# A graph-transformer layer: mixer coefficients taken four pairs at a time, closing blocks reordered, TensorE loops in the first stage, two table comparisons on GpSimd

## The chip, the cores and the metric

One core of one Trainium2 chip runs the whole program. The metric is the device time in microseconds of one execution, the median of the runs. Before the change it is 474.52 us (three runs, 474.12 to 474.85). The profiler took one further execution: it took 474.66 us, and its span from first to last instruction is 472.9 us.

## The reference, cut to what matters

N = 384 nodes, D = 1024 features, 16 heads of 64, 12288 edges. All tensors are float32. Three blocks are computed from the same normalised input:

```python
xn = layernorm(x)
# 1: graph attention
q, k, v = xn @ wq.T + bq, xn @ wk.T + bk, xn @ wv.T + bv
q2, k2, v2 = heads(q @ wiq.T + biq), heads(k @ wik.T + bik), heads(v @ wiv.T + biv)
mask = full((N, N), -inf); mask[src, dst] = softplus(w)[type - 1]; mask[i, i] = w3 where it is -inf
attn = softmax(q2 @ k2.T / 8 + mask)
gnn = (attn @ v2) @ wo.T + bo
# 2: mixer
f(x) = exp(-x * x / 2)
coeff = sum over the 64 columns of a head of f(xn @ Wq + bq) * f(xn @ Wk + bk)
mix = (coeff * (xn @ Wv + bv)) @ Wo + bo
# 3: feed-forward with one chosen expert, on layernorm(x + gnn + mix)
```

## The kernel before, in words

Every float32 product is made of three TensorE products of rounded halves: high part of the weights by high part of the data, high by low, low by high. ScalarE makes the high part of a weight block (`split_hi`), VectorE the low part (`split_weights`), and SyncE loads the blocks (512 KB each) into a ring of slots (`load_weights`). A semaphore for each slot says that its high part is there (`hi_ready`), its low part (`lo_ready`), and that TensorE is done with it (`w_used`).

TensorE works through a fixed order of jobs, written out by hand:

- The first stage has 32 column jobs (`column_job`: 24 matmuls of 128x128 by 128x384): q, k, v from the input, then q2. Each job takes one slot of four and one PSUM bank of four, and waits for its bank (`bank_free`), `hi_ready` and `lo_ready`. All of it is unrolled. ScalarE and VectorE empty the banks; VectorE also looks for double edges, and GpSimd scatters the edge values into four tables in DRAM (`tables`).
- The v2 stage has eight row blocks and one column job for k2. At its end the four tables come back into SBUF: table 0 becomes the mask, and VectorE merges the other three into it (`merge_table`: a comparison of 1152 columns that finds the entries present, then a predicated copy).
- Eight pairs of heads follow (`pair(j)` on ScalarE and VectorE, the loop over j on TensorE). TensorE does `scores(j)` (18 matmuls with 64 rows), `pv(j-1, 0)` (6 matmuls), three column jobs in banks 0 and 1, `pv(j-1, 1)`, the column job of the mixer's values (`rv`), and `coefficients(j)`: two matmuls of a block matrix of ones (`head_ones`) by the high and the low part of the features, into bank 0. The features of a pair are one tensor: ScalarE squares q and k of the mixer (`square`), VectorE adds them, ScalarE takes exp (line 702) and its high part (704), VectorE the low part (1103). ScalarE empties the value job (`mix_value`, 718), VectorE multiplies by the coefficients in PSUM (1108), ScalarE and GpSimd split the product into the halves `T2` (733 and 469). The last scores of a pair wait for `mix_value`, the `pv` for the low part of the turned probabilities (`turned_lo`, 1041), and the first column job of the pair for the product (`mix_ready`), since it uses bank 0.
- The closing stage has two halves of eight row blocks. In each the blocks b = 0 to 3 take the mixer's data (`T2`), 4 to 7 the attention's (`T0`). Block 0 of the first half lies inside the last pair, and `pv(7, 0)` and `pv(7, 1)` lie behind blocks 1 and 2. SyncE loads the four first blocks of the feed-forward weights (`E_USES`) between these, and GpSimd loads x again (509).
- The feed-forward stage and the output follow, which the change leaves as they are.

## Time and profile before

| what | value |
|---|---|
| median of 3 runs | 474.52 us (474.12 to 474.85) |
| profiled execution | 474.66 us, span 472.9 us |
| TensorE matmul busy | 465.9 us (99%) |
| VectorE busy | 342.3 us (72%) |
| ScalarE busy | 262.2 us (55%) |
| GpSimd busy | 157.2 us (33%) |
| granted TensorE clock | 1.000 |
| DMA | 91.92 MB, 194 GB/s |

The page gives the busy time of each engine and a chain of work followed back from the last instruction. The end of a matmul is modelled, so two neighbouring matmuls overlap in the record: what one costs is the distance of the starts, not its duration. An idle time stands in brackets behind a row, with what ended it.

### The profile page before, as it was taken

Reading aid. Unit: us, or ns where it says so; the run is one execution under the profiler, and the core shown is the slowest. Engines: PE = TensorE matmul, PEld = TensorE weight load, DVE = VectorE, ACT = ScalarE, POOL = GpSimd, SP = SyncE. Lnnn points to the kernel's source line nnn. Section 1 sums busy time; section 2 is a strip of 40 time slices with the busy share of each in tenths; the row PEclk is TensorE's granted clock in tenths of the full one; section 3 lists DMA queues with packets and bytes.
Section 4 is the critical chain, followed back from the end, with each engine's and each line's share of the span. In section 5 each row is a group of like instructions: output and inputs, shape, how many; then the busy total and the mean of one; then the engine's idle time right before and its main releaser. Section 6 shows DMA issues by size and latency. Waiting matters only on the chain.

```text
span 472.9 us, 7361 instructions
## 1 busy us (share of the span) xinstructions
PE 465.9 (99%) x2533; PEld 432.4 (91%) x2533; DVE 342.3 (72%) x796; ACT 262.2 (55%) x429; POOL 157.2 (33%) x176
## 2 busy tenths in 40 slices
PE   7999999999999999999999999999999999999996
PEld 5999999999999888999999999999998888888885
DVE  6979966677626259687978888796966794587294
ACT  3734433333324245788989889897974542163170
POOL 3147677777767741002130202212142000050200
PEclk9999999999999999999999999999999999999999
DMA  8877756655444454577675766766679835210463
GB/s 243 325 230 230 239 195 167 176 182 180 154 152 153 133 200 179 175 226 253 205 232 184 235 192 197 247 180 224 192 240 382 308 115 179 89 46 0 155 247 133
DMA packets 39049, 91.92 MB, mean 194 GB/s; under 512 B 7410, under 2 KB 20306, under 8 KB 38884
## 3 DMA queue, kind: packets, MB, share of 16 engines
q1 hardware_dynamic: 33604, 83.15, 54.0%
q0 software_dynamic: 4832, 7.45, 4.7%
q10 hardware_dynamic: 576, 0.85, 0.5%
q8 instruction: 20, 0.33, 0.3%
q14 instruction: 17, 0.14, 0.1%
HBM read 77.96 MB, written 13.47 MB: 193 GB/s over the span
## 4 chain that ended last, share of the span: by engine, by line
PE 87%; DVE 5%; DMA 3%; ACT 3%; issue 1%; SPq 0%; DVEq 0%; ACTq 0%
PE PS L1278 32%; PE PS L1288 28%; PE PS L1283 16%; PE PS L1416 3%; PE PS L1404 2%; DMA turn<-U 2%; PE PS L1535 2%; PE PS L1346 2%; DMA U<-x 1%; DVE U L1076 1%; DVE w_lo L895 1%; PE PS L1266 1%; ACT U L659 1%; PE PS L1539 1%; ACT w_hi L536 1%
## 5 line engine op out<-in xcount | busy, mean ns | idle before, releaser
L895 DVE TENSOR_TENSOR w_lo<-raw,w_hi 128x1024 fp32r<-128x1024 f32 x86 | 104.4, 1225 | 45.0 <-ACT w_hi L536 45.0
L536 ACT ACTIVATE w_hi<-raw 128x1024 fp32r<-128x1024 f32 x87 | 90.8, 1054 | 68.5 <-PE PS L1288 44.1
L454 POOL DMA_INDIRECT table<-evalue,where x96 | 103.0, 1073 | 45.7 <-issue 25.2
L1283 PE MATMUL PS<-xT_hi,w_lo 128*128 128x384 f32 x320 | 61.9, 334 | 0.0
L1278 PE MATMUL PS<-xT_hi,w_hi 128*128 128x384 f32 x320 | 61.9, 334 | 0.0
L1278 PE MATMUL PS<-xT_lo,w_hi 128*128 128x384 f32 x320 | 61.9, 334 | 0.0
L1278 PEld LDWEIGHTS PS<-xT_lo,w_hi 128*128 128x128 f32 x320 | 56.0, 188 | 0.0
L1278 PEld LDWEIGHTS PS<-xT_hi,w_hi 128*128 128x128 f32 x320 | 56.0, 188 | 0.0
L1283 PEld LDWEIGHTS PS<-xT_hi,w_lo 128*128 128x128 f32 x320 | 56.0, 188 | 0.0
L469 POOL TENSOR_TENSOR T_lo<-U,T_hi 128x384 fp32r<-128x384 f32 x8 | 8.2, 1020 | 97.8 <-ACT T_hi L733 97.8
L1288 PE MATMUL PS<-w_hi,T_hi 128*128 128x512 f32 x144 | 40.0, 391 | 0.0
L1288 PE MATMUL PS<-w_hi,T_lo 128*128 128x512 f32 x144 | 39.8, 389 | 0.0
L950 DVE SCALAR_TENSOR_TENSOR U<-U,V,cst 128x128 f32<-128x128 f32 x96 | 33.6, 350 | 6.0 <-DMA U<-key_dram 3.7
L1288 PE MATMUL PS<-w_lo,T_hi 128*128 128x512 f32 x144 | 37.8, 389 | 0.0
L598 ACT ACTIVATE T_hi<-PS,bias 128x384 fp32r<-128x384 f32 x24 | 13.8, 576 | 41.7 <-PE PS L1283 41.7
L1288 PEld LDWEIGHTS PS<-w_hi,T_lo 128*128 128x128 f32 x144 | 27.0, 188 | 5.7
L1288 PEld LDWEIGHTS PS<-w_lo,T_hi 128*128 128x128 f32 x144 | 27.0, 188 | 5.6
L1288 PEld LDWEIGHTS PS<-w_hi,T_hi 128*128 128x128 f32 x144 | 27.0, 188 | 5.2
L1076 DVE STREAM_TRANSPOSE U<-U 128x384 f32<-128x384 f32 x48 | 24.0, 551 | 10.5 <-DMA turn<-U 10.5
L659 ACT ACTIVATE U<-U,nmax 128x384 f32<-128x384 f32 x48 | 28.9, 605 | 3.7 <-DVE nmax L1064 3.7
L965 DVE SCALAR_TENSOR_TENSOR T_lo<-PS,bias,T_hi 128x384 fp32r<-128x384 f32 x24 | 14.8, 615 | 16.1 <-ACT T_hi L598 16.1
L666 ACT ACTIVATE U<-U,rsum 128x384 f32<-128x384 f32 x48 | 25.8, 604 | 0.0
(241 smaller groups left out, 817.1 us busy)
## 6 DMA issues: line engine op xcount, KB each, us to landing
raw<-weights SPq DMA_DIRECT2D x84, 512.0 KB, 4.6
turn<-U SPq DMA_DIRECT2D x16, 576.0 KB, 4.0
U<-turn SPq DMA_DIRECT2D x64, 144.0 KB, 2.9
U<-key_dram SPq DMA_DIRECT2D x32, 192.0 KB, 4.1
mask<-weights SPq DMA_DIRECT2D x9, 512.0 KB, 5.1
table<-Q POOLq DMA_DIRECT2D x4, 576.0 KB, 9.5
V<-conv SPq DMA_DIRECT2D x4, 512.0 KB, 5.4
U<-table POOLq DMA_DIRECT2D x3, 576.0 KB, 7.5
```

The lines of the kernel that those rows point to most:

```text
L454: pool.indirect_dma_start(tables[g], bass.IndirectOffsetOnAxis(ap=where[:, k:k + 1], axis=0), evalue[:, k:k + 1], None, bounds_check=N * N ...
L536: act.activation(w_hi[slot][:], raw[slot][:], ACT.Copy).then_inc(hi_ready[slot], 1)
L659: act.activation(prob[:, h, t, :], prob[:, h, t, :], ACT.Exp, bias=nmax[:, h, t:t + 1], scale=SCALE, accum_out=ssum[:, h, t:t + 1]).then_i ...
L666: act.activation(prob[:, h, t, :], prob[:, h, t, :], ACT.Copy, scale=rsum[:, h, t:t + 1]).then_inc(prob_ready, 1)
L895: dve.tensor_tensor(w_lo[slot][:], raw[slot][:], w_hi[slot][:].bitcast(F32), ALU.subtract).then_inc(lo_ready[slot], 1)
L950: dve.scalar_tensor_tensor(out=key_junk, in0=key_row[:, s, c * P:(c + 1) * P], scalar=ekey[:, ch0 + c:ch0 + c + 1], in1=tri, op0=ALU.is_eq ...
L965: dve.scalar_tensor_tensor(out=dst[1][:, j, :], in0=PS[:, A_BANKS[a % 4], 0:N], scalar=bias[:, a:a + 1], in1=dst[0][:, j, :].bitcast(F32), ...
L1076: dve.transpose(blocks.rearrange("p (c m t i) -> p t m c i", c=NQ, m=NT, t=NT)[:, t], prob[:, h, t, :].rearrange("p (m c i) -> p m c i", m ...
L1278: pe.matmul(o, w_hi[slot][:, k * P:(k + 1) * P], src[part][:, k, :], start=(k == 0 and part == 0), stop=False)
L1283: last = pe.matmul(o, wl, src[0][:, k, :], start=False, stop=(k == KB - 1))
L1288: return pe.matmul(bank, src[part][:, 2 * kp + k2, t * P:(t + 1) * P], weights_in[slot][:, k2 * HALF:(k2 + 1) * HALF], start=start, stop=stop)
L1416: last = pe.matmul(PS[:, 7, 0:N], vs[:, m, h, :], probT[part][:, m, :], start=(m == 0 and part == 0), stop=(m == NT - 1 and part == 1))
```

## The change

1. The coefficients are computed for four pairs at once (`GROUP` = 4). The mixer's columns (Wq, Wk, Wv, their biases, and the rows of Wo) are laid out in another order on the host, so that a block of 128 columns holds 16 columns of each of eight heads, and four blocks hold eight heads whole. VectorE adds up the features of the four blocks (`feat_sum`), and `head_ones` has groups of 16 in place of 64. High part, low part and the two matmuls are done for j = 3 and j = 7 alone. The values of the pairs are kept (`raw_value`), and VectorE multiplies all four in a row behind the coefficients. The splits of the products come four pairs later, the last four in the closing stage.
2. In the closing stage the first half takes its blocks in another order, the feed-forward weights are loaded and split two blocks later, behind a wait for all of the mixer's products, and GpSimd loads x ahead of the last four low parts.
3. Jobs 4 to 31 of the first stage are two loops on TensorE with four jobs in the body (five rounds and two), whose waits compare with a register.
4. The comparisons for tables 1 and 2 are done on GpSimd (`is_gt` for `not_equal`), into two buffers. VectorE keeps that of table 3 and the three predicated copies.

```diff
+GROUP = 4
+SHARE = HD // GROUP
+C_ORDER = (((1, 0), (1, 1), (0, 0), (0, 1), (0, 2), (1, 2), (1, 3), (0, 3)),
+           ((1, 0), (1, 1), (1, 2), (1, 3), (0, 0), (0, 1), (0, 2), (0, 3)))
...
+        feat_sum = v2_rows[:, :, 0:P]
+        def raw_value(j):
+            return v2_rows[:, :, j * P:(j + 1) * P] if j else mix_v.rearrange(rows_of_three, t=NT)
...
             for b in range(5, 16):
                 load_weights(*C_USES[b], weights[72 + b])
-                if b == 5:
-                    sp.wait_ge(vs_ready, KB)
                 if b == 7:
+                    sp.wait_ge(ml_ready, KB)
                     sp.wait_ge(score_read, KB * 6 + 1)
-                if 5 <= b < 9:
-                    load_weights(*E_USES[(b - 5)], weights[72 + 16 + (b - 5)])
+                if 7 <= b < 11:
+                    load_weights(*E_USES[(b - 7)], weights[72 + 16 + (b - 7)])
...
+            for g in range(STREAMS - 2):
+                pool.wait_ge(table_in[g], 16)
+                if g == 0:
+                    pool.wait_ge(dup_ready, CH)
+                if g == 1:
+                    pool.wait_ge(diag_step, 2 * NT)
+                pool.tensor_scalar(present[g], later[g], ABSENT, None, ALU.is_gt).then_inc(found, 1)
...
             for j in range(KB):
-                if j:
+                if j >= GROUP:
                     pool.wait_ge(vs_ready, j)
-                    mix_lo(j - 1)
-                    pool.wait_ge(ml_ready, j)
+                    mix_lo(j - GROUP)
+                    pool.wait_ge(ml_ready, j - GROUP + 1)
                 values(j)
...
                 normalise(1)
+                if j >= GROUP:
+                    mix_hi(j - GROUP)
                 if j:
-                    mix_hi(j - 1)
-                    act.wait_ge(feat_ready, j)
+                    act.wait_ge(feat_exp, j)
+                if j > 1:
+                    act.wait_ge(feat_added, adds(j - 1))
                 square(sq_q, 1, 6, rq)
...
                 act.wait_ge(sq_summed, j + 1)
-                act.activation(sq_q, sq_q, ACT.Exp, scale=-0.5).then_inc(feat_exp, 1)
-                act.wait_ge(feat_exp, j + 1)
-                act.activation(feat[0], sq_q, ACT.Copy).then_inc(feat_hi, 1)
+                if j == 0:
+                    act.wait_ge(vs_ready, 1)
+                if j == GROUP:
+                    act.wait_ge(feat_ready, 1)
+                act.activation(sq_q.rearrange(rows_of_three, t=NT) if j % GROUP else feat_sum,
+                               sq_q.rearrange(rows_of_three, t=NT), ACT.Exp, scale=-0.5).then_inc(feat_exp, 1)
                 split_hi(*ahead[3])
+                if j % GROUP == GROUP - 1:
+                    act.wait_ge(feat_added, adds(j))
+                    act.activation(feat[0].rearrange(rows_of_three, t=NT), feat_sum, ACT.Copy).then_inc(feat_hi, 1)
                 turned_hi(j, 0)
+                mix_value(j, rv)
                 if j:
                     out_hi(j - 1)
-                mix_value(j, rv)
...
             for j in range(KB):
                 pair(j)
-            mix_hi(KB - 1)
             split_hi(*C_USES[2])
             split_hi(*C_USES[3])
             pv_copy(KB - 1, 0)
             turned_hi(KB - 1, 1)
+            for j in range(KB - GROUP, KB):
+                mix_hi(j)
             split_hi(*C_USES[4])
...
             def merge_table(g):
-                dve.wait_ge(table_in[g], 16)
-                dve.tensor_scalar(present, later[g], ABSENT, None, ALU.not_equal).then_inc(mask_step, 1)
-                dve.wait_ge(mask_step, 2 * g + 1)
+                if g < STREAMS - 2:
+                    dve.wait_ge(found, g + 1)
+                else:
+                    dve.wait_ge(table_in[g], 16)
+                    dve.tensor_scalar(present[0], later[g], ABSENT, None, ALU.not_equal).then_inc(found, 1)
+                    dve.wait_ge(found, g + 1)
...
-                dve.wait_ge(feat_hi, j + 1)
-                dve.tensor_tensor(feat[1], sq_q, feat[0].bitcast(F32), ALU.subtract).then_inc(feat_ready, 1)
+                if j % GROUP:
+                    dve.wait_ge(feat_exp, j + 1)
+                    if adds(j) > 1:
+                        dve.wait_ge(feat_added, adds(j) - 1)
+                    dve.tensor_tensor(feat_sum, feat_sum, sq_q.rearrange(rows_of_three, t=NT),
+                                      ALU.add).then_inc(feat_added, 1)
                 split_weights(*ahead[3])
+                if j % GROUP == GROUP - 1:
+                    dve.wait_ge(feat_hi, j // GROUP + 1)
+                    high, low = (f.rearrange(rows_of_three, t=NT) for f in feat)
+                    dve.tensor_tensor(low, feat_sum, high.bitcast(F32), ALU.subtract).then_inc(feat_ready, 1)
                 turned_lo(j, 0)
-                dve.wait_ge(coeff_done, j + 1)
-                dve.wait_ge(mixv_ready, j + 2)
-                dve.tensor_tensor(mix_v, PS[:, 0, 0:N], mix_v, ALU.mult).then_inc(mix_ready, 1)
+                if j % GROUP == GROUP - 1:
+                    dve.wait_ge(coeff_done, j // GROUP + 1)
+                    dve.wait_ge(mixv_ready, j + 2)
+                    for i in range(j - GROUP + 1, j + 1):
+                        dve.tensor_tensor(raw_value(i), PS[:, 0, 0:N].rearrange(rows_of_three, t=NT), raw_value(i),
+                                          ALU.mult).then_inc(mix_ready, 1)
...
-            for a in range(2, FIRST):
-                pe.wait_ge(bank_free[a % 4], a // 4 + 1)
-                column_job(*A_USES[a], T0 if a >= 3 * KB else xT, A_BANKS[a % 4])
+            for a in (2, 3):
+                pe.wait_ge(bank_free[a], 1)
+                column_job(*A_USES[a], xT, A_BANKS[a])
+            for src, begin, end in ((xT, 1, 3 * KB // 4), (T0, 3 * KB // 4, FIRST // 4)):
+                with pe.Fori(0, end - begin) as i:
+                    for s in range(4):
+                        pe.wait_ge(bank_free[s], i + (begin + 1))
+                        column_job(A_SLOTS[s], i + begin, src, A_BANKS[s])
...
-                    pe.wait_ge(mix_ready, j + 1)
+                    if j % GROUP == 0:
+                        pe.wait_ge(mix_ready, j + 1)
+                    else:
+                        pe.wait_ge(sq_done, 2 * j)
                     column_job(*slot_use(rk), T1, 0)
...
-                pe.wait_ge(sq_done, 2 * j + 2)
-                coefficients(j)
+                if j % GROUP == GROUP - 1:
+                    pe.wait_ge(sq_done, 2 * j + 2)
+                    coefficients(j)
...
-                    pe.wait_ge(ol_ready if b >= 4 else ml_ready, 2 * (b % 4) + 2)
-                    row_block(*uses[b], T2 if b < 4 else T0, banks, b % 4, b == 0, b == 7)
+                    mixer, kp = C_ORDER[half][b]
+                    pe.wait_ge(ml_ready if mixer else ol_ready, 2 * kp + 2)
+                    row_block(*uses[b], T2 if mixer else T0, banks, kp, b == 0, b == 7)
```

## Rows read from the trace of the kernel before

**Rows 1.** Part 1 of the page: busy time, share of the span, instructions.
```profile
PE 465.9 (99%) x2533; PEld 432.4 (91%) x2533; DVE 342.3 (72%) x796; ACT 262.2 (55%) x429; POOL 157.2 (33%) x176
```

**Rows 2.** Stretches: length, busy time of each engine, clock, DMA share, GB/s.
```profile
23.00:147.00 124.00, 124.00 (x716) 123.74 (x715) 88.01 (x281) 46.37 (x61) 85.77 (x80) 1.00 0.61 188
...
203.75:225.25 21.50, 21.29 (x130) 20.53 (x130) 18.65 (x43) 19.09 (x37) 2.67 (x4) 1.00 0.70 227
225.25:246.30 21.05, 21.05 (x129) 20.55 (x128) 17.70 (x42) 18.23 (x36) 4.37 (x5) 1.00 0.68 215
...
330.52:351.86 21.34, 21.23 (x123) 19.90 (x123) 17.57 (x41) 18.11 (x36) 4.49 (x5) 1.00 0.68 217
```

**Rows 3.** One line's instructions: least, median, greatest duration in ns, first and last start.
```profile
L1425 PE MATMUL PS<-T_lo,head_ones x8: 338/338/339, 203.5 to 351.7; 128*128 128x384 f32 x8
```

**Rows 4.** Timeline around the end of pair 3: start us, duration us, engine, line.
```profile
242.41 0.53 ACT L702 ACTIVATE U<-U 128x384 f32<-128x384 f32 x1
...
243.40 1.05 ACT L536 ACTIVATE w_hi<-raw 128x1024 fp32r<-128x1024 f32 x1
...
244.48 1.23 DVE L895 TENSOR_TENSOR w_lo<-raw,w_hi 128x1024 fp32r<-128x1024 f32 x1 [0.39 <-ACT w_hi L536]
...
245.62 1.35 DVE L1041 TENSOR_TENSOR probT_lo<-U,probT_hi 128x1152 fp32r<-128x1152 f32 x1
...
246.04 0.34 PE L1425 MATMUL PS<-T_lo,head_ones 128*128 128x384 f32 x1
...
246.06 0.58 ACT L718 ACTIVATE U<-PS,bias 128x384 f32<-128x384 f32 x1
...
247.01 0.56 DVE L1108 TENSOR_TENSOR U<-PS,U 128x384 f32<-128x384 f32 x1
...
247.46 0.35 PE L1404 MATMUL PS<-T_hi,q_hi 64*128 64x384 f32 x2
...
247.49 0.55 DVE L1060 CUSTOM_DVE_ANT_0 U<-PS,mask 128x384 f32<-128x384 f32 x1
...
249.24 1.55 PE L1278 MATMUL PS<-T_hi,w_hi 128*128 128x384 f32 x8
```

**Rows 5.** Timeline at the start of pair 7, where TensorE waits twice.
```profile
331.96 0.18 PEld L1404 LDWEIGHTS PS<-T_hi,q_hi 64*128 64x128 f32 x2 [0.44 <-ACT U L718]
...
332.69 0.19 PEld L1416 LDWEIGHTS PS<-probT_hi,vs 128*128 128x128 f32 x1 [0.26 <-DVE probT_lo L1041]
```

**Rows 6.** Merge of the tables: timeline rows, two lines' durations, landings of the tables.
```profile
179.09 0.75 DVE L986 TENSOR_SCALAR U<-U 128x1152 f32<-128x1152 f32 x1
...
184.64 1.55 DVE L988 COPY_PREDICATED mask<-U 128x1152 f32<-128x1152 uint32 x1
...
190.82 1.55 PE L1278 MATMUL PS<-xT_hi,w_hi 128*128 128x384 f32 x8
...
L485 POOL CAST vs<-V x8: 503/503/1260, 185.6 to 347.7; 128x384 fp32r<-128x384 f32 x8
...
DMA to landing us min/median/max: 5.0/7.1/10.1
```

**Rows 7.** First stage: a sequencer's wait, chain, fetch queue, two small transfers to landing.
```profile
L1275 PEldq EVENT_SEMAPHORE  x1: 51/51/51, 36.5 to 36.5; - x1
...
39.78 2.77 PE PS L1278 x16
...
q8 instruction: 20, 0.33, 0.3%
...
U<-down_b SPq DMA_DIRECT2D x1, 0.2 KB, 2.4
...
bias<-bias_cols SPq DMA_DIRECT2D x1, 36.0 KB, 4.3
```

**Rows 8.** Closing stage: last low part of the attention, a weight split that waits.
```profile
364.22 1.01 POOL L476 TENSOR_TENSOR T_lo<-U,T_hi 128x384 fp32r<-128x384 f32 x1 [7.69 <-ACT T_hi L738]
...
369.07 1.06 ACT L536 ACTIVATE w_hi<-raw 128x1024 fp32r<-128x1024 f32 x1 [3.65 <-DMA raw<-weights]
```

More of the change, by code:

```diff
@@ L58, with adds @@
 DEPTH = len(A_SLOTS) - 1
+def adds(j):
+    return j - j // GROUP
 def slot_use(r):
@@ L132, in gps_layer @@
         later = [U[:, g * NT * N:(g + 1) * NT * N].rearrange("p (t n) -> p t n", t=NT) for g in range(STREAMS - 1)]
-        present = U[:, 4608:4608 + NT * N].rearrange("p (t n) -> p t n", t=NT)
+        present = [U[:, c:c + NT * N].rearrange("p (t n) -> p t n", t=NT) for c in (3456, 4608)]
         prob = U[:, 0:2 * NT * N].rearrange("p (h t n) -> p h t n", h=2, t=NT)
@@ L250, in gps_layer @@
         mask_step = sem("mask_step")
+        found = sem("found")
         v_copied = sem("v_copied")
@@ L277, in gps_layer @@
         feat_exp = sem("feat_exp")
+        feat_added = sem("feat_added")
         feat_hi = sem("feat_hi")
@@ L464, in _ @@
                     table_in[g - 1] if g else first_mask_in, 16)
+            for g in range(STREAMS - 2):
[5 more added lines that the diff above has]
+                pool.tensor_scalar(present[g], later[g], ABSENT, None, ALU.is_gt).then_inc(found, 1)
             def mix_lo(j):
                 pool.wait_ge(mh_ready, j + 1)
-                pool.tensor_tensor(T2[1][:, j, :], mix_v, T2[0][:, j, :].bitcast(F32),
+                high, low = (T2[c][:, j, :].rearrange(rows_of_three, t=NT) for c in range(2))
+                pool.tensor_tensor(low, raw_value(j), high.bitcast(F32),
                                    ALU.subtract).then_inc(ml_ready, 1)
@@ L502, in _ @@
                     pool.dma_start(row_bo, rows[0:2, :].partition_broadcast(P)).then_inc(rows_in, 16)
-            mix_lo(KB - 1)
-            pool.wait_ge(ml_ready, KB)
             pool.wait_ge(pT_ready, KB * 2 - 1)
             pool.wait_ge(block_ready, KB * 6)
-            pool.wait_ge(feat_ready, KB)
+            pool.wait_ge(feat_ready, KB // GROUP)
             pool.dma_start(x_rows, x.rearrange("(t p) d -> p t d", p=P)).then_inc(xr_in, 16)
+            for j in range(KB - GROUP, KB):
+                mix_lo(j)
+                pool.wait_ge(ml_ready, j + 1)
             out_lo(KB - 1)
@@ L714, in mix_value @@
                 act.wait_ge(w_used[slot], use + 2)
-                if j:
-                    act.wait_ge(ml_ready, j)
-                act.activation(mix_v, PS[:, 1, 0:N], ACT.Identity,
+                act.wait_ge(vs_ready, j + 1)
+                act.activation(raw_value(j), PS[:, 1, 0:N].rearrange(rows_of_three, t=NT), ACT.Identity,
                                bias=bias[:, 8 * KB + j:8 * KB + j + 1]).then_inc(mixv_ready, 1)
@@ L732, in mix_hi @@
                 act.wait_ge(mix_ready, j + 2)
-                act.activation(T2[0][:, j, :], mix_v, ACT.Copy).then_inc(mh_ready, 1)
+                act.activation(T2[0][:, j, :].rearrange(rows_of_three, t=NT), raw_value(j),
+                               ACT.Copy).then_inc(mh_ready, 1)
             def out_hi(j):
@@ L747, in _ @@
             turned_hi(KB - 1, 1)
+            for j in range(KB - GROUP, KB):
+                mix_hi(j)
             split_hi(*C_USES[4])
@@ L766, in _ @@
                 split_hi(*C_USES[b])
-                if 6 <= b < 10:
-                    split_hi(*E_USES[b - 6])
+                if 8 <= b < 12:
+                    split_hi(*E_USES[b - 8])
                 if b == 10:
@@ L1152, in _ @@
                     add_rows(1)
-                if 6 <= b < 10:
-                    split_weights(*E_USES[b - 6])
+                if 8 <= b < 12:
+                    split_weights(*E_USES[b - 8])
                 if b == 9:
@@ L1566 @@
     v2, k2 = halves(a["gnn_wiv"].T), columns(a["gnn_wik"].T)
-    mixer = [columns(a["mix_" + n]) for n in ("Wq", "Wk", "Wv")]
+    lane = np.arange(P)
+    turned = np.concatenate([(2 * GROUP * (j // GROUP) + lane // SHARE) * HD + SHARE * (j % GROUP) + lane % SHARE
+                             for j in range(KB)])
+    mixer = [columns(a["mix_" + n][:, turned]) for n in ("Wq", "Wk", "Wv")]
     pairs = [v2[0:4], k2[0:1], v2[4:8]]
@@ L1571 @@
     pairs += [mixer[n][KB - 1:KB] for n in (1, 0, 2)]
-    wo, mo = halves(a["gnn_wo"].T), halves(a["mix_Wo"])
-    outs = [mo[0:4], wo[0:4], mo[4:8], wo[4:8]]
+    wo, mo = halves(a["gnn_wo"].T), halves(a["mix_Wo"][turned])
+    outs = [(wo, mo)[mixer][4 * half + kp:4 * half + kp + 1] for half in range(2) for mixer, kp in C_ORDER[half]]
     weights = np.concatenate(first + pairs + outs + [halves(a["ffn_base_W"].T)])
@@ L1596 @@
         "disc": disc.transpose(3, 0, 1, 2),
-        "bias_cols": np.concatenate([a[n].reshape(KB, P) for n in names]).T,
+        "bias_cols": np.concatenate([(a[n][turned] if n.startswith("mix") else a[n]).reshape(KB, P)
+                                     for n in names]).T,
         "rows": np.stack([a["gnn_bo"], a["mix_bo"], a["ffn_base_b"]]),
```

14 lines of the change are left out of this document (7 added, 7 removed).

## The prediction

> **What bounds the kernel now.** I read the busy times first: TensorE works for 465.9 of 472.9 us [rows 1]; the next engine is VectorE with 72%. Then the stretches. In the whole unrolled first stage TensorE is never idle (124.00 of 124.00), and a regular pair of heads, from its first score matmul to that of the next, takes 21.05 us with no idle time [rows 2]. Two pairs are longer, 21.50 and 21.34 us. The timeline shows why: at the start of pair 7 TensorE waits 0.44 us for the emptied value bank (line 718) and then 0.26 us for the low part of the turned probabilities (line 1041) [rows 5]; pair 1 begins with the same two waits, shorter ones (two borders of eight). So the kernel is bound by the number of matmuls, with some tenths lost at two borders. An edit gains if it takes matmuls away, and gains nothing if it only relieves another engine; it loses when it makes TensorE wait.
>
> **Part 1, grouped coefficients.** Two matmuls of each of the 16 go away for six of eight pairs: 12 matmuls. The line with the low features has eight of them, of 338 ns [rows 3], but these overlap: sixteen matmuls of the same shape take 2.77 us in the chain, 0.173 us each [rows 7]. 12 x 0.173 = 2.08 us, all on TensorE's path, since nothing hides there. Gain 2.08 us.
>
> What the removed matmuls covered: the scores now start 0.35 us earlier after the value job, and their last third waits for line 718, the `pv` for line 1041. At the border of pairs 3 and 4 line 718 begins at 246.06 and is done at 246.64, and the last third of the scores begins at 247.46: 0.8 us of slack, 0.5 when TensorE comes 0.35 earlier. Line 1041 ends at 246.97, and the six matmuls of the `pv` before the column job of 249.24 begin near 248.1, 1.1 us behind that [rows 4]. So in the regular pairs nothing is late. At pairs 1 and 7 the `pv` already waits for line 1041. That line comes earlier as well: ScalarE no longer copies the high features (between exp and the split of 243.40 [rows 4]) ahead of the weight split that VectorE's split and line 1041 stand behind. Both sides move by 0.35 and about 0.45 us, so 0.1 us is regained at each border: 0.2 us. Bounds: nothing, or the whole excess of these pairs over 21.05, 0.45 + 0.29 = 0.74 us [rows 2].
>
> The groups' ends, j = 3 and 7. The feature chain is longer there: VectorE adds (as long as the 0.56 of line 1108), ScalarE splits the weights and then copies, VectorE splits the weights and then takes the low part. With the rows of pair 3 [rows 4]: ScalarE's split can begin when exp ends, 242.94 in place of 243.40, and ends about 243.95; its copy ends 244.5; VectorE's split, which waits for ScalarE's, runs from 244.0 to 245.2, the low part to 245.7. The second coefficient matmul starts at 246.04: in time by 0.3 us. Line 1041 then runs to 247.0 as before. The four products come at a distance of 0.48 us (247.01 to 247.49): three more are 1.45 us, the last ends at 247.01 + 1.45 + 0.56 = 249.0. TensorE's next column job overwrites the coefficients' bank at 249.24. So it is in time by 0.2 us; at a distance of 0.62 us (one duration and a little) it would wait 0.2 us. I take 0.1 us lost. Queued behind the four products on VectorE is the read of the next scores (line 1060), which begins 1.45 us later; the job that needs those banks starts 4.2 us behind the one at 249.24, so it isn't late. At j = 7 the products stand before the closing blocks, which now want them far later.
>
> VectorE's and ScalarE's work per pair (17.7 and 18.2 of 21.05 us [rows 2]) does not grow: six additions replace six low parts, six copies go.
>
> **Part 2, closing stage.** No matmul is added or taken away. The mixer's blocks 2 and 3 move behind three attention blocks. The last products are ready about 249.0 - 246.04 = 3 us behind the last coefficients; ScalarE takes four high parts only after the splits and `turned_hi` there, and GpSimd four low parts of 1.0 to 1.8 us, the last of them about where the attention's last low part ran before, 364.22 [rows 8]. In the new order the first block that wants them starts 4 x 4.1 us + two `pv` of 1.0 us behind block 1, near 370. SyncE's four loads for the feed-forward come two blocks later. That relieves the stretch in which a split waited 3.65 us for its weights [rows 8], a wait that TensorE didn't feel; the four are needed 45 us later. Behind SyncE's new wait for all products (near 364) stands the load for block 8, needed near 382. I cost all this at nothing; the cover is 5 us at the tightest.
>
> **Part 3, the loops.** The same 28 jobs. The three waits of a job become instructions with registers on TensorE's sequencer. They were satisfied long before, since slots and banks turn over in four jobs. What hides the sequencer's work is its lead: the wait of a job ran at 36.5 us, the job's matmuls began at 39.78 [rows 7], 3.3 us later. Register steps and a branch fit in that lead if the instructions are at hand. I take 0; the other end is a rival below.
>
> **Part 4, comparisons on GpSimd.** VectorE's merges begin at 179.09 and end with the third copy, 184.64 + 1.55 = 186.2; the three comparisons of 0.75 and three copies of 1.55 us fill that time [rows 6]. GpSimd takes 0.50 us for a cast of 384 columns, 1.26 us when it is held up, so 1.5 to 3.8 us for 1152 columns [rows 6]. With 1.5 the entries are found at 180.6 and 182.1, the copies follow, the third table has landed by 173.1 + 10.1 = 183.2, and the merge ends near 186.0. No change; TensorE wants the score banks at 190.82 [rows 6], and six reads of 0.5 us (the distance of line 1060) behind 186.2 end at 189.3. The two comparisons removed from VectorE lie in slack: below nothing this can't go.
>
> The Trainium skill (SBUF — State Buffer, "Practical consequences") says that a VectorE instruction with two SBUF inputs contends with a GpSimd instruction that reads SBUF, and that one of the two blocks fully. The spread of the cast, 503 to 1260 ns, agrees with it [rows 6]; a serial order of these pieces would end the merge 1.5 us later than I wrote, which the slack of 1.5 us nearly covers.
>
> **The sum.** -2.08 - 0.2 + 0.1 = -2.2 us. The profiled execution took 474.66 us (span 472.9): 472.5 us. The median is 0.14 us lower: 472.4 us. About 0.2%, 0.95 us, is what a measurement of this kernel can tell from no change.
>
> **Rival A: the loops fetch again (ends slower).** The instructions come in through a queue of their own: 20 packets, 0.33 MB, so 16 KB each, which is about 256 instructions [rows 7]. One round of the loop has 4 x 48 matmul and weight-load instructions and some 20 others. If the jump back finds its target gone, the sequencer stands until a block has come. A round straddles a border of such blocks in most positions. The price of one fetch: the smallest transfer lands after 2.4 us, one of 36 KB in the busy beginning after 4.3 [rows 7]; a block's packet itself takes 0.3% x 16 x 472.9 / 20 = 1.1 us more. That is 3.5 to 5.4 us, of which the lead hides 3.3. There are five jumps back (4 and 1): 1 to 10 us. At 4.3 us a fetch it is 5.0 us, and the time is 477.4 us. It decides from a fetch of 3.3 us on, and makes the kernel slower than before from 3.8 us. For it: size of body and block, and the trace has no slack in this stage. Against it: the lead, and that nothing here shows whether a block just left stays. It would show as five gaps on TensorE between 31 and 147 us and more packets in that queue.
>
> The Trainium skill (Runtime: NRT & Kernel Launch, "Instruction fetch mechanics") has this rule: prefetch is sequential, and a taken branch to a target outside the two blocks at hand waits for a DMA of it. It also gives TensorE's memory as 2048 instructions, by which the whole body would stay. The page thus speaks for both; no row of before has a branch.
>
> **Rival B: the mask comes late.** If GpSimd needs 2.6 us for a comparison, held up by the copies, entries are found at 181.7 and 184.3 and the merge ends at 188.2, 2 us late. The six reads of scores (0.5 us each) end at 191.3; TensorE waits 0.4 us, and the turned probabilities of pair 0, for which TensorE waited already, come about 1 us later: +1.5 us, 473.9 us. At 3.8 us a comparison TensorE alone waits 3.0 us, 475.4. For it: no slack for VectorE there; against it: the tables' early landing.
>
> **Rival C: the matmuls go and TensorE waits instead.** If the slack of 0.3 us at the ends of the groups or of 0.5 at the borders isn't there, since the strided features and values cost more or the turned probabilities come back late, each border gives back up to 0.35 us. Half of them: +1.0 us, 473.4 us. The rows of pairs 1 and 7 speak for it, the regular pairs against.
>
> **How the numbers follow.** Forecast 0.54, own range 471.6 (the whole 0.74 regained) to 473.1 (nothing regained, 0.5 lost at the groups' ends). Rival A 0.24: mostly slower (0.17), partly within (0.05). Rival B 0.11: mostly within. Rival C 0.11: faster 0.07, within 0.04. Together faster 0.62, within 0.2% 0.19, slower 0.19. The range goes up into rival A to 476.8, which leaves about 0.12 above it and 0.04 below.
>
> **What would show it.** Right: TensorE idle-free from 23 to 147 us; pairs of 20.7 us for j = 0, 1, 2, 4, 5, 6 and four coefficient matmuls in all; the fourth product done before the first column job of pair 4; block 5 of the closing stage without a wait. Wrong: five gaps in the first stage; a merge that ends behind 187.5; TensorE idle before line 1278 at the start of pair 4.

## The result, and the profile after

The changed kernel takes 480.31 us (median of four runs, 478.77 to 483.87), the kernel before 474.33 us beside it: ratio 1.0114, 95% interval 1.0062 to 1.0166. The forecast was 472.4 us with a range up to 476.8, so it was wrong in sign and the time lies outside the range. The ratios here and below are those of the fast executions alone (within 1.5% of the kernel's fastest), so they need not be the ratios of the medians. The profiled execution took 479.62 us, its span is 477.8 us.

Part 1 of the page, and one group of part 5 (busy us and mean ns of one, then the idle time before it):

```profile
PE 464.7 (97%) x2521; PEld 431.2 (90%) x2521; DVE 344.8 (72%) x794; ACT 257.8 (54%) x423; POOL 164.7 (34%) x178
...
L1334 PE MATMUL PS<-xT_hi,w_hi 128*128 128x384 f32 x320 | 63.3, 339 | 4.2 <-DVE smax L1105 4.2
```

TensorE has 12 instructions fewer than in [rows 1], as the change says. But its busy share fell from 99 to 97%: the work went, the time didn't. Nearly all of the new idle time is one wait, for the scores of pair 0. The waits of TensorE (line waited for, total, times, longest):

```profile
PE PS L1334 <- DVE smax L1105: 4.2, 1, 4.2
PE PS L1381 <- DVE w_lo L893: 1.6, 1, 1.6
PE PS L1322 <- ACT U L595: 1.4, 1, 1.4
PE PS L1339 <- DVE probT_lo L937: 0.9, 1, 0.9
...
PE PS L1466 <- ACT U L758: 0.5, 1, 0.5
PE PS L1478 <- DVE probT_lo L1086: 0.2, 1, 0.2
```

The second, third and fourth lie in the first 31 us, and waits at these places stand in most profiles, with and without the change (before has the second and 0.7 us of the third). The timeline of the merge answers to [rows 6]; first GpSimd's instructions with their durations, then VectorE's, then TensorE's:

```profile
L490 POOL TENSOR_SCALAR U<-U x2: 3837/4155/4473, 179.5 to 183.4; 128x1152 f32<-128x1152 f32 x2
...
183.35 1.57 DVE L1033 COPY_PREDICATED mask<-U 128x1152 f32<-128x1152 uint32 x1 [3.03 <-POOL U L490]
187.97 1.88 DVE L1033 COPY_PREDICATED mask<-U 128x1152 f32<-128x1152 uint32 x1 [3.05 <-POOL U L490]
189.89 1.42 DVE L1031 TENSOR_SCALAR U<-U 128x1152 f32<-128x1152 f32 x1
191.34 1.52 DVE L1033 COPY_PREDICATED mask<-U 128x1152 f32<-128x1152 uint32 x1
...
196.15 2.93 PE L1334 MATMUL PS<-xT_hi,w_hi 128*128 128x384 f32 x8 [4.16 <-DVE smax L1105]
198.88 1.66 PE L1334 MATMUL PS<-xT_lo,w_hi 128*128 128x384 f32 x8
```

A comparison takes GpSimd 3.84 and 4.47 us, not 1.5. VectorE stands idle before the first two copies, which wait for GpSimd; the mask is whole at 192.9 us (186.2 before), six reads of scores follow, and TensorE starts again at 196.15. There its first eight matmuls lie 2.73 us apart from the next eight; at full clock that distance is 1.39 us. So a second loss of 1.4 us follows the wait: the granted clock is at its lower level (0.50, 1.2 GHz) behind the idle time. Stretches, with length, busy time of the engines, clock, DMA share and GB/s, the last of them that of the first eight matmuls:

```profile
31.00:158.00 127.00, 127.00 (x721) 125.40 (x721) 88.05 (x277) 48.25 (x64) 93.17 (x87) 1.00 0.61 183
185.78:210.21 24.43, 20.27 (x115) 19.44 (x115) 16.00 (x37) 14.74 (x29) 4.77 (x3) 0.93 0.33 108
210.21:231.96 21.75, 21.03 (x127) 20.15 (x126) 18.34 (x41) 17.97 (x34) 2.19 (x2) 1.00 0.73 230
231.96:252.65 20.69, 20.69 (x127) 20.19 (x126) 17.80 (x42) 17.21 (x34) 2.83 (x3) 1.00 0.70 220
252.65:273.69 21.04, 21.04 (x129) 20.54 (x128) 18.43 (x42) 17.95 (x35) 2.54 (x3) 1.00 0.70 223
...
196.15:198.88 2.73, 2.73 (x8) 2.73 (x9) 2.73 (x6) 2.73 (x10) 0.00 (x0) 0.50 0.16 29
```

The first row is the stretch of the loops: no gap. The next four are pairs 0 to 3, each from its first score matmul to that of the next. Pair 0 is 5.46 us longer than before (18.97), pair 1 0.25 longer, pair 2 0.36 shorter, pair 3 even, pairs 4 to 6 0.3 shorter each, and what follows 0.43 shorter. With 1.00 us by which pair 0 starts later, that is the +5.0 us between the two traces.

### The profile page after: what moved, and what is told of

It reads as the page before. It is cut to its first block, busy times and chain, and to the rows that moved or that the text cites. A ratio compares the mean times of both kernels' runs of the same rounds, so it can differ in the third digit from the quotient of the medians.

```text
span 477.8 us, 7358 instructions
## 1 busy us (share of the span) xinstructions
PE 464.7 (97%) x2521; PEld 431.2 (90%) x2521; DVE 344.8 (72%) x794; ACT 257.8 (54%) x423; POOL 164.7 (34%) x178
## 4 chain that ended last, share of the span: by engine, by line
PE 66%; DMA 12%; issue 8%; POOL 7%; DVE 5%; ACT 0%; POOLq 0%; DVEq 0%; SPq 0%; ACTq 0%
PE PS L1334 24%; PE PS L1344 21%; PE PS L1339 12%; DMA table<-evalue,where 7%; POOL table L471 5%; PE PS L1478 4%; PE PS L1466 2%; POOL U L490 2%; PE PS L1602 2%; DMA turn<-U 1%; DMA key_dram<-V 1%; DVE w_lo L937 1%; DMA raw<-weights 1%; DMA U<-x 1%; DMA U<-key_dram 1%
## 5 line engine op out<-in xcount | busy, mean ns | idle before, releaser
L1334 PE MATMUL PS<-xT_hi,w_hi 128*128 128x384 f32 x320 | 63.3, 339 | 4.2 <-DVE smax L1105 4.2
L1334 PEld LDWEIGHTS PS<-xT_hi,w_hi 128*128 128x128 f32 x320 | 57.1, 191 | 4.5 <-DVE smax L1105 4.5
L512 POOL CAST vs<-V 128x384 fp32r<-128x384 f32 x8 | 5.7, 717 | 75.7 <-PE PS L1478 75.7
```

The source lines that it names most:

```text
L1334: pe.matmul(o, w_hi[slot][:, k * P:(k + 1) * P], src[part][:, k, :], start=(k == 0 and part == 0), stop=False)
```

## The experiments

The experiments ran on five chips. On three of them TensorE is held up in the first stage whatever the kernel: its matmuls come at multiples of 0.7 us for some 20 us, with nothing that the trace shows it to wait for, and the medians of all kernels lie between 496 and 504 us, that of before too. The first eight kernels and the last two ran there. Their total times tell little; their traces do.

### Each part by itself

e1 is the changed kernel with all comparisons on VectorE, e4 also without the loops; e2 is the kernel before with the two comparisons on GpSimd, e3 with the loops.

```diff
  e1, e4 (against after; e4 also has the 28 jobs unrolled)
-                pool.tensor_scalar(present[g], later[g], ABSENT, None, ALU.is_gt).then_inc(found, 1)
...
+                dve.tensor_scalar(present[1], later[g], ABSENT, None, ALU.not_equal).then_inc(found, 1)
  e2 (against before): the same lines the other way round
  e3 (against before)
+            for src, begin, end in ((xT, 1, 3 * KB // 4), (T0, 3 * KB // 4, FIRST // 4)):
+                with pe.Fori(0, end - begin) as i:
```

> The changed kernel with part 4 undone alone: all three comparisons on VectorE again; grouping, closing order and loops stay. Theory M (the mask comes late because a GpSimd comparison takes 3.8 to 4.5 us, and everything that is lost follows from it): the wait of 4.2 us and the half clock behind it go, pair 0 takes about 18.6 us, and the time is 474.3 - 2.1 = 472.2 us, 0.4 to 0.5% below before. Theory L (the loops or the regrouped work also cost time): above 473.5 us.

> The kernel before with part 4 alone: two comparisons on GpSimd, nothing else. Theory M: TensorE waits about 4 us in pair 0, a stretch at half clock follows, and the time is 474.3 + 8.1 = 482 us (480 to 485), with a wide spread. Theory L: a clearly smaller loss, under 3 us, since the rest of the loss would belong to the other parts.

> The kernel before with part 3 alone: 28 jobs of the first stage in two loops on TensorE. Theory M: no gap between the jobs and 474.3 us within 0.1%, with about four packets fewer in the instruction queue. Theory L (each jump back costs time that the one trace did not show): 1 us or more above before.

> Parts 1 and 2 alone: grouped coefficients and the closing order, with the first stage unrolled and the comparisons on VectorE. Theory M: 472.2 us, the same as with the loops. Theory L: faster than the version with loops by what the loops cost. Predicted sum of my steps: 474.3 - 2.2 = 472.1 us.

Ratios to before: e1 1.0099 (1.0039 to 1.0158), e2 0.997 (0.9903 to 1.0037), e3 1.0037 (0.9979 to 1.0095), e4 1.0031 (0.9972 to 1.009). The two theories can't be told apart by these. Taken at their word, the comparisons would be harmless and the rest would cost time. The trace of e1 says why that can't be read so:

```profile
98.27 0.33 PE L1322 MATMUL PS<-xT_lo,probT_hi 128*128 128x384 f32 x1 [0.42 <-issue]
99.00 0.34 PE L1327 MATMUL PS<-xT_hi,probT_lo 128*128 128x384 f32 x1 [0.39 <-issue]
...
PE PS L1322 <- issue: 12.9, 16, 2.0
```

TensorE reaches pair 0 at 204 to 211 us in these runs in place of 185. VectorE's work ahead of the merge comes late with it, and GpSimd's two comparisons are done by then: in e2 at 189.4 and 198.9 us, while VectorE's first copy begins at 199.63 without waiting for GpSimd. The mask is whole at 205.08 us, 1.1 us behind the start of pair 0 (before: 1.4 us), and e2's pair 0 takes 18.97 us, as before, in spite of its comparisons. What does come through is part 1: pairs 2 and 6 take 20.69 to 20.94 us in e1 and e4 and 21.05 to 21.07 us in e2 and e3.

### The same again, matmuls in the gap, one comparison

e5 and e6 repeat e1 and e2. e7 is the changed kernel with 24 matmuls more (4.16 us) where TensorE waited; e8 moves one comparison to GpSimd and not two.

```diff
  e7
+                    if j == 0:
+                        for _ in range(24):
+                            pe.matmul(PS[:, 7, 0:N], head_ones[:], T1[0][:, 0, :], start=True, stop=True)
  e8
-            for g in range(STREAMS - 2):
+            for g in range(STREAMS - 3):
```

> The changed kernel with all three comparisons on VectorE, once more, since on the first chip every kernel, the one before too, lost some 20 us in the first stage at half rate and times could not be told apart. Theory M (all that is lost follows from the late mask): 472.2 us where before takes 474.3, 0.4 to 0.5% faster. Theory L (the loops or the regrouped work cost too): no faster than before.

> The kernel before with the two comparisons on GpSimd alone, once more. Theory M: about 8 us over before (6 to 10), with TensorE waiting about 4 us for the score reads of pair 0. On the first chip pair 0 took 18.97 us, as before, because TensorE came to it 19 us later, and the mask was there: by theory M that is so wherever TensorE is late, by theory L it would be a sign that the comparisons are harmless.

> The changed kernel with 24 more matmuls of 128x128 by 128x384 (4.16 us) into an unused bank where TensorE waits in pair 0; their results are not used. If the half clock behind the wait follows from TensorE's idle time, the clock stays at full and the time falls by 1.4 us or more below the changed kernel, to about 478 us, with a narrower spread, although there is more work. If the clock falls for another reason, the time stays at 480.

> The changed kernel with one comparison on GpSimd (table 1) and two on VectorE. A comparison of 3.8 us ends at 183.3; copy, comparison, copy, comparison, copy on VectorE end near 188.8 in place of 192.9. TensorE then waits about 1.5 us for the score reads. Theory M: 473.5 to 475.5 us, between the version with none (472.2) and the one with two (480). Theory L (the loss is not in the mask): 480.

The medians are 502.72, 502.06, 499.12 and 497.35 us beside 503.82 (484.78 to 507.35) for before: nothing to be told apart, and the gap that e7 was to fill wasn't there. Its pairs 0 and 1 take 22.81 and 20.69 us: 18.65 + 4.16, and no wait at the border of pair 1; that this is so because ScalarE and VectorE had 4 us more is argued, not shown. In e8 the single comparison took 3.56 us:

```profile
189.24 3.56 POOL L490 TENSOR_SCALAR U<-U 128x1152 f32<-128x1152 f32 x1 [4.51 <-DMA U<-table]
```

### The start of the merge held back

To make the lateness a matter of choice, g1 and g2 hold GpSimd's first comparison until the second or third v2 block of the second half is done, d1 does it with VectorE's merge of e1, and f2 is g2 with 36 matmuls more (6.24 us) in the gap. These ran where TensorE was mostly undisturbed (before 479.29 us, 473.95 to 484.52).

```diff
  g2 (g1: V2_JOBS[1][1]; d1: the same wait on dve)
+                if g == 0:
+                    gate_slot, gate_use = slot_use(V2_JOBS[1][2])
+                    pool.wait_ge(w_used[gate_slot], gate_use + 2)
  f2: g2 and the matmuls of e7, range(36)
```

> The chips of the last runs lose 10 to 30 us in the first stage in every kernel, so that TensorE comes to pair 0 long after the tables. Here the mask's lateness is put back relative to TensorE: in the changed kernel the first GpSimd comparison also waits for the end of the third of the last four v2 blocks, 4.1 us before the scores of pair 0. In the changed kernel's first trace the comparisons began 6.3 us before the scores and TensorE waited 4.2 us, with 16.7 us from the first comparison to the restart. Theory M: restart at -4.1 + 16.7 = 12.6 us behind the scores where 6.0 is natural, a wait of 6.5 us, half clock behind it, and a pair 0 of 26 us in place of 18.6. Theory L: pair 0 under 20 us.

> The same, with the first comparison waiting for the second of the last four v2 blocks, 8.2 us before the scores. Theory M: a wait of 2.4 us, pair 0 of 21 to 22.5 us, that is 4 us less than with the later gate, one for one with the gate. Theory L: no difference between the two gates.

> The later gate (4.1 us before the scores) with all three comparisons on VectorE. Merges of 7.1 us and reads of 3.2 us end 6.3 us behind the scores, where 6.0 is natural. Theory M: a wait of at most 0.5 us and a pair 0 of about 19 us at full clock: the engine that compares decides, not when the tables are there. If the lateness of the tables mattered by itself, pair 0 would be as long as with the comparisons on GpSimd.

> The later gate on GpSimd with 36 more matmuls (6.24 us) into an unused bank in the wait; their results are not used. If the half clock comes from TensorE's idle time, pair 0 takes 18.6 + 6.5 = 25.1 us at full clock and the restarted job's first eight matmuls keep a distance of 0.173 us, against 0.32 to 0.34 and 26.4 us without the filler. If not, both are alike.

Measured: g2 484.42 us, ratio 1.0159 (1.01 to 1.0219); g1 481.75, 1.0091 (1.0048 to 1.0135); d1 477.58, 0.9992 (0.9951 to 1.0033); f2 480.02, 1.0044 (1.0004 to 1.0083). d1 is as fast as before although its TensorE waits 1.3 us for the mask and 1.4 us for a weight split behind VectorE's late work: what parts 1 to 3 give is used up by it. In the profiles of d1 and f2 the added wait does bind (the first comparison begins 3.9 and 3.8 us ahead of pair 0's scores, where the gate was set). In those of g1 and g2 it doesn't: the tables landed later still. The row names the transfer as the releaser:

```profile
183.30 8.14 POOL L493 TENSOR_SCALAR U<-U 128x1152 f32<-128x1152 f32 x2 [4.24 <-DMA U<-table]
...
199.48 2.93 PE L1337 MATMUL PS<-xT_hi,w_hi 128*128 128x384 f32 x8 [7.49 <-DVE smax L1108]
202.21 2.28 PE L1337 MATMUL PS<-xT_lo,w_hi 128*128 128x384 f32 x8
204.33 1.57 PE L1342 MATMUL PS<-xT_hi,w_lo 128*128 128x384 f32 x8
```

So both profiles are repeats of the changed kernel in an execution where the tables came late, the two gates can't be compared as meant, and the wait is 7.5 us (7.6 in g1). The 16 matmuls behind it take 4.85 us in place of 2.77, a loss of 2.1 us to the lower clock. f2 tests just that: with 6.24 us of matmuls more its median is 4.4 us below g2's, and TensorE restarts at full clock and without a wait:

```profile
191.95 6.40 PE L1517 MATMUL PS<-T_hi,head_ones 128*128 128x384 f32 x36
198.19 1.57 PE L1337 MATMUL PS<-xT_hi,w_hi 128*128 128x384 f32 x8
199.60 1.55 PE L1337 MATMUL PS<-xT_lo,w_hi 128*128 128x384 f32 x8
```

The lower clock comes from the idle time: with the gap filled the granted clock stays at 1.00. How much of the 4.4 us is the clock and how much the earlier tables of f2's executions this pair doesn't separate.

### The parts once more, on a chip that was not held up

The changed kernel, e1, e4 and e2 again, side by side; before took 477.83 us (474.73 to 482.6, 29 runs).

> The changed kernel itself, beside its parts on one chip. Theory: the comparisons on GpSimd cost 4.2 us of idle TensorE time at the start of pair 0 and 1.4 us of halved clock behind it, the grouped coefficients give 2.1 us back, and some tenths are lost at pair 1. Expected 478 to 480 us where before takes 474.3, 3.5 to 5 us above before on the same chip. Rival (the one slow read of one execution): the loss is another one in each execution, and the time stands within 2 us of before.

> Changed kernel with the comparisons of tables 1 and 2 back on VectorE, all else kept. Theory (part 4 alone makes the loss): 2 to 2.5 us below before on the same chip, some 472.3 us, where TensorE works undisturbed; and 5.5 to 7 us below the changed kernel. Rival (grouping delays the tables or pair 1 as well): 473.5 to 475 us, nothing gained over before.

> Only the grouped coefficients and the reordered closing blocks: no loops, comparisons on VectorE. Theory: loops are worth nothing either way, so within 0.5 us of the kernel with loops. Rival A (loops wait for instructions): 1 to 10 us faster than the kernel with loops.

> The kernel before with the two comparisons moved to GpSimd and nothing else. Theory: the wait of 4.2 us ahead of the first probability-side column job of pair 0 and the halved clock behind it come alone, so 5 to 6.5 us above before, about 480 us. Rival (the wait needs the grouping, whose pair 0 is shorter by 0.35 us): under 1 us above before.

| kernel | median us (runs) | ratio to before | tables asked for at | mask whole at | wait | pairs 0 to 3 |
|---|---|---|---|---|---|---|
| before (first profile) | 474.52 (3) | | 170.7 | 186.2 | 0 | 82.58 |
| after (first profile) | 480.31 (4) | 1.0114 (1.0062 to 1.0166) | 173.0 | 192.9 | 4.2 | 87.91 |
| h1, all parts | 481.25 (12) | 1.0072 (1.0032 to 1.0111) | 175.6 | 195.6 | 8.0 | 92.25 |
| h2, comparisons back | 476.16 (12) | 0.9969 (0.9924 to 1.0015) | 173.3 | 187.5 | 0 | 85.67 |
| h3, parts 1 and 2 alone | 474.33 (12) | 0.9953 (0.9909 to 0.9997) | 174.7 | 191.8 | 4.3 | 87.04 |
| h4, comparisons alone | 483.16 (6) | 1.0112 (1.0056 to 1.0168) | 176.3 | 196.9 | 7.8 | 92.10 |

The last four columns come from the profile of each, one execution. The rows for h4, and for h3, where VectorE does all three comparisons:

```profile
176.26 0.82 POOL L464 DMA_DIRECT2D mask<-table  x1 [1.88 <-DMA table<-evalue,where]
...
183.80 8.33 POOL L474 TENSOR_SCALAR U<-U 128x1152 f32<-128x1152 f32 x2 [4.41 <-DMA U<-table]
...
200.18 2.93 PE L1291 MATMUL PS<-xT_hi,w_hi 128*128 128x384 f32 x8 [7.83 <-DVE smax L1073]
```

```profile
174.66 0.80 POOL L480 DMA_DIRECT2D mask<-table  x1 [1.86 <-DMA table<-evalue,where]
...
183.96 0.75 DVE L1019 TENSOR_SCALAR U<-U 128x1152 f32<-128x1152 f32 x1
184.75 1.57 DVE L1021 COPY_PREDICATED mask<-U 128x1152 f32<-128x1152 uint32 x1
186.35 0.90 DVE L1019 TENSOR_SCALAR U<-U 128x1152 f32<-128x1152 f32 x1
187.29 2.24 DVE L1021 COPY_PREDICATED mask<-U 128x1152 f32<-128x1152 uint32 x1
...
195.07 2.93 PE L1322 MATMUL PS<-xT_hi,w_hi 128*128 128x384 f32 x8 [4.31 <-DVE smax L1093]
```

Three things follow. The comparisons alone make the whole loss: h4 is 5.3 us above before (2.7 to 8.0), and taking them back from h1 to h2 gives 5.1 us. Parts 1 and 2 without them are faster than before, by 2.2 us (0.1 to 4.3): the amount forecast, if with a wide interval, and h3 beats both kernels. (With the loops as well, h2's gain can't be told from none, and its median of 476.2 us missed the 472.3 expected.) And the merge had no slack to give in the first place: GpSimd asks for the tables, behind its last scatters, at 170.7 us in the profile of before and at 173 to 176 us in the others. From there the mask takes 14.1 to 17.1 us with VectorE's comparisons and 19.9 to 20.6 with GpSimd's. h3's execution came late enough that TensorE waited 4.3 us without any comparison on GpSimd. The runs of before on this chip stand in two groups, 15 from 474.7 to 477.8 and 14 from 479.6 to 482.6 us, about the price of that wait and its clock. The mean granted clock of the runs divides them in the same way: 0.998 to 1.000 in the 15, 0.991 to 0.996 in the 14; the profiled execution of h3, with its wait, has 0.995. I take the late tables for the cause, but no profile of such a run of before was made. What makes the scatters end early or late stays open.

The groups also tell what the parts do. h3's runs divide likewise, seven from 472.6 to 474.4 us (clock 0.998 to 1.000) and five from 477.2 to 479.6 (0.993 to 0.995). Their medians, 474.0 and 478.2, lie 1.9 and 2.5 us below those of before, 475.9 and 480.7: the gain of parts 1 and 2 is there in either group, and isn't a matter of how many runs fell into which. And all 18 runs of h1 and h4 have a clock of 0.996 or less: with the comparisons on GpSimd every execution shows the mark of the wait, without them (before, h2, h3) 20 of 53 do. The first comparison of the two kernels was made against four runs of before that all lie at 474.1 to 474.9 us, which would explain that its distance, 6.0 us, is larger than the one here, 3.4.

Lateness that doesn't show as a wait for the mask comes out at the borders: h2 has none of the first, but pairs 1 to 3 take 22.1 to 22.3 us. Pairs 1 and 2 wait 0.9 us each for the emptied value bank, pair 3 waits 0.8 us at its second coefficient matmul, and h1 has that last wait too. A row of h2, pair 1, then one of h1, pair 3:

```profile
206.91 0.45 PE L1454 MATMUL PS<-T_hi,q_hi 64*128 64x384 f32 x2 [0.91 <-ACT U L749]
```

```profile
276.53 0.44 PE L1487 MATMUL PS<-T_lo,head_ones 128*128 128x384 f32 x1 [0.81 <-DVE T_lo L1157]
```

### What a comparison costs GpSimd, and the loops again

i1 is e3 again. i2 is the kernel before with twelve GpSimd operations more in the closing stage.

```diff
+            for n in (1152, 384):
+                src, dst = U[:, 3840:3840 + n], U[:, 4992:4992 + n]
+                step_m(pool.tensor_scalar(dst, src, ABSENT, None, ALU.is_gt))
+                step_m(pool.tensor_scalar(dst, src, ABSENT, None, ALU.mult))
+                step_m(pool.tensor_copy(dst, src))
+                step_m(pool.tensor_tensor(dst, src, src, ALU.subtract))
+                step_m(pool.memset(dst, 0.0))
+                step_m(pool.tensor_scalar(dst, src, ABSENT, None, ALU.is_gt))
```

> The kernel before with the loops alone. Theory: the loops cost and give nothing, TensorE has no gap from 32 to 147 us, four packets fewer in the instruction queue; time within 1 us of before on the same chip. Rival (the median of the kernel with loops stood 1.8 us above that of the one without): 1 to 2 us above before, with idle time of TensorE or later starts of the scatters on GpSimd.

> The kernel before with twelve more GpSimd operations in the closing stage, where GpSimd has nothing to do: comparison, multiplication by a constant, copy, subtraction, memset, comparison, each on 1152 and then on 384 columns of SBUF. Theory (a comparison costs GpSimd some 3.8 us for 1152 columns by itself, as any operation with arithmetic does; a cast is not a measure of it): comparisons of 3.8 us and 1.3 us, multiplication the same, copy 1.2 to 1.5 us and 0.5 us. Rival (VectorE held GpSimd up in the merge): a comparison of 1.5 us here, where VectorE is idle for long.

Both ran on a chip that holds TensorE up, so i1 (501.75 us beside 498.57, 480.85 to 502.47) settles nothing on time; it has 16 packets of instructions, as every kernel with the loops. i2, by line, busy us and mean ns:

```profile
L529 POOL TENSOR_SCALAR U<-U 128x1152 f32<-128x1152 f32 x1 | 4.0, 4010 | 0.1
L525 POOL TENSOR_SCALAR U<-U 128x1152 f32<-128x1152 f32 x1 | 3.8, 3770 | 0.1
L524 POOL TENSOR_SCALAR U<-U 128x1152 f32<-128x1152 f32 x1 | 3.2, 3156 | 0.1
L527 POOL TENSOR_TENSOR U<-U 128x1152 f32<-128x1152 f32 x1 | 3.0, 2961 | 0.1
...
L524 POOL TENSOR_SCALAR U<-U 128x384 f32<-128x384 f32 x1 | 1.8, 1787 | 0.1
L526 POOL COPY U<-U 128x1152 f32<-128x1152 f32 x1 | 1.8, 1782 | 0.1
```

A comparison of 1152 columns takes 3.2 to 4.0 us, a multiplication as long, a subtraction 3.0, a copy 1.8. The rival of 1.5 us is out. VectorE was busy beside them, so these aren't GpSimd's times undisturbed. f2 has one that is: VectorE was idle from 181.43 us on, and the first comparison, begun at 182.07, took 3.15 us. First f2's two comparisons and VectorE's rows about the first, then the row of the changed kernel just ahead of its own:

```profile
L493 POOL TENSOR_SCALAR U<-U x2: 3148/3798/4447, 182.1 to 185.3; 128x1152 f32<-128x1152 f32 x2
...
180.20 1.23 DVE L940 TENSOR_TENSOR w_lo<-raw,w_hi 128x1024 fp32r<-128x1024 f32 x1
185.25 1.54 DVE L1036 COPY_PREDICATED mask<-U 128x1152 f32<-128x1152 uint32 x1 [3.83 <-POOL U L493]
...
179.09 1.23 DVE L937 TENSOR_TENSOR w_lo<-raw,w_hi 128x1024 fp32r<-128x1024 f32 x1
```

What goes beyond 3.15 us is time for which VectorE was already at work. In the changed kernel its weight split still had 0.84 us to run when the first comparison began, and its predicated copy 1.52 us when the second did: these took 3.84 and 4.47 us, 0.7 and 1.3 more than 3.15. h1 and h4 show the same (3.77 and 3.79 us beside 0.77 and 0.80 us left of the split, 4.46 beside the copy). So 6.3 of the 8.3 us are GpSimd's own, and 2.0 are VectorE in its way.

## Why the prediction was wrong

**The step that failed** is the duration in part 4: "So 1.5 to 3.8 us for 1152 columns. With 1.5 the entries are found at 180.6 and 182.1". They were found at 183.3 and 187.9. Of the 5.8 us by which the second is late, 5.3 are the two durations (3.3 GpSimd's own price, 3.15 us in place of 1.5 each, and 2.0 the time behind VectorE's split and copy), 0.4 the later landing. The copy behind it and the last comparison, slower beside GpSimd (1.88 and 1.42 us against 1.55 and 0.75), add 1.1, so the mask is whole at 192.9 in place of 186.0. The price was taken from the cast of 384 columns, a moving operation, when a row with arithmetic of the same engine and width stood among my own: the subtraction of 1.01 us [rows 8], three times which is 3.0. Even the upper end, 3.8, was too low for the second comparison.

**Rival B was the right mechanism, priced too low.** At 3.8 us a comparison it gave a wait of 3.0 and 475.4 us. The wait was 4.2, though TensorE wanted the banks only at 191.99 us, 1.2 later than I had read; the clock behind it, which I had not in the sum, took 1.4; and its chance of 0.11 rested on tables that land as early as in the one profile. In other executions they are asked for up to 5.6 us later, and the wait is 8 us. That the comparisons "lie in slack" was read from a single execution of a chain that hangs on 96 indirect transfers.

**Part 1 held.** Pairs 2, 4 and 6 take 20.69 to 20.73 us against 21.05, the 2 x 0.173 us of the step; pair 3 takes 21.04 with no wait at its second coefficient matmul, so the 0.1 us for the groups' ends was not lost here, though 0.8 was in h1 and h2. The 20.7 us that I listed for pair 0 too was a slip: that pair took 18.97 us before, and takes 18.62 in e4 and e5. At pair 1 nothing was regained: it waits 0.67 and 0.35 us for the value bank and the turned probabilities (the 0.5 and 0.2 of the list, and the overlap of neighbouring records) where I had 0.1 us less wait than before. From the first score matmul of pair 7 the rest of the kernel takes 141.92 us, 0.43 less than before (142.35); but the kernels with the old coefficients and closing order (e2, h4) take 141.92 and 141.93 us there too. So that gain is the border's wait of [rows 5], absent in all the other profiles of the old order, and not a gain of the change.

**Part 2 held.** The same stretch takes 141.90, 141.91 and 141.91 us in h1, h2 and h3, against 141.93 in h4: the order of the blocks is worth nothing either way.

**Part 3 held as far as traces go, and rival A fell.** TensorE is idle-free from 31 to 158 us, and the queue of instructions has fewer packets, not more:

```profile
q8 instruction: 16, 0.26, 0.2%
```

Against 20 and 0.33 MB in [rows 7]. The five jumps back fetched nothing that this count shows. The Trainium skill (Runtime: NRT & Kernel Launch, "Instruction fetch mechanics") has two statements on this, and the larger memory that it gives for TensorE fits; by its rule of two blocks at hand alone, jumps from one block back over a border could have shown as packets and gaps, and the trace shows neither. The medians of h2 and h3 stand 1.8 us apart with overlapping intervals, so a cost of the loops of a microsecond isn't excluded by time.

**Rival C** is real as a way in which lateness comes out (h2's pairs, h1's group end), but in the changed kernel it took 0.6 us at pair 1 alone.

**The start of pair 0**, 1.00 us later, is none of the change: it lies between 184.56 and 186.14 us in the ten traces of undisturbed first stages, 185.53 and 184.65 in two with the loops, 184.56 and 186.14 in two without them. It goes with a wait at 31 us that some executions have (0.9 us here): the three traces without it begin pair 0 at 184.56 to 184.78 us, the seven with it, 0.6 to 1.4 us long, at 185.53 to 186.14.

## What to carry to other kernels

Price an operation that changes engine by a row of the same engine and the same kind of work; between ends a factor of 2.5 apart, a copy is not the nearest row to arithmetic. Where work moves onto the chain behind a transfer, look at that transfer's landing in more than one execution before calling anything slack: two comparisons of 0.75 us on VectorE, with VectorE free, became 8.3 us in series on GpSimd, 2.0 of them spent behind VectorE's own instructions. And a wait of a few microseconds on the bound engine costs more than itself, since the clock falls behind it.

## What the runs showed of the hardware

- GpSimd took 3.15 us for a float32 comparison of 128x1152 with VectorE idle (f2), 3.1 to 4.5 us over all runs (1.55 to 1.8 for 384 columns in i2), VectorE 0.75 us. An instruction of VectorE with two inputs that is under way makes it longer (above), and VectorE's are longer beside GpSimd's too. In i2 its subtraction of 128x1024, 1.22 us by itself, took 3.88 us when it began with GpSimd's comparison:

```profile
385.06 3.16 POOL L524 TENSOR_SCALAR U<-U 128x1152 f32<-128x1152 f32 x1
...
385.19 3.88 DVE L913 TENSOR_TENSOR w_lo<-raw,w_hi 128x1024 fp32r<-128x1024 f32 x1 [1.89 <-ACT w_hi L554]
```

  The Trainium skill (SBUF — State Buffer, "Practical consequences") says that such a pair contends, and that in VectorE's two-port modes the other side is blocked wholly. The sizes here agree with a full block: VectorE's subtraction ends 0.85 us behind the comparison, 2.7 us late, and in e2 and e7 two that began during a comparison took 2.5 us and ended 0.8 us behind it.
- Behind an idle time of 4.2 and 4.3 us (after, h3) TensorE lost 1.4 us to the lower clock, behind 7.5 to 8.0 us (g1, g2, h1, h4) 1.9 to 2.2 us, and none when matmuls without use filled the gap (f2).
- On three of the five chips TensorE's matmuls came at multiples of 0.7 us for 15 to 23 us, beginning between 63 and 110 us, and in nine of the ten profiles for some further microseconds later. The granted clock fell only 3 to 10 us after this had begun, so it isn't what starts it. It costs some 20 to 30 us on the total, for all kernels alike, with a cause that the traces don't show.
